# A graph layer on one core: two of three node pairs turned by VectorE, their blocks fetched in eight transfers, the straight pairs normalised by VectorE

## The reference

```python
msg = x[src]
agg = segment_sum(msg, dst, n)
deg = segment_sum(1, dst, n)
mean = agg / max(deg, 1)[:, None]
h = mean @ W_l + b + x @ W_r
u = x + h * sigmoid(h)
out = (u - mean(u)) / sqrt(var(u) + 1e-5)      # over a row's 512 features
```

## Time and profile before

| | |
|---|---|
| median of 3 runs (lowest to highest) | 1550.5 us (1549.07 to 1550.78) |
| the profiled execution: its own time, its span | 1550.07 us, 1548.2 us |
| mean granted TensorE clock | 0.989 of 2.4 GHz |
| busy shares of the span: PE, DVE, ACT, POOL | 97%, 85%, 77%, 67% |
| moved by DMA, mean rate | 397.68 MB, 257 GB/s |

### The profile page before, as it was taken

One profiled execution on the slowest core, in us unless ns is written; L12 is line 12 of the kernel. 1 busy time (PEld: TensorE's weight loads), 2 busy tenths in 40 slices (PEclk: granted clock), 3 DMA queues, 4 the chain that ended last, 5 costly groups with the idle time before them and its releaser, 6 DMA issues.

```text
span 1548.2 us, 23957 instructions
## 1 busy us (share of the span) xinstructions
PE 1501.8 (97%) x7198; PEld 1244.3 (80%) x7198; DVE 1319.6 (85%) x2088; ACT 1184.4 (77%) x1609; POOL 1030.7 (67%) x1097
## 2 busy tenths in 40 slices
PE   7799999999999899999999999999999999999996
PEld 6687778888887787888888888888888888888884
DVE  7699999999998777888888888888888888888886
ACT  4354433333334698999999999999999999999996
POOL 6466556656662766667767777677677776776673
PEclk9899999999999999999999999999999999999998
DMA  5656589989997689999999999999999999999995
GB/s 193 173 178 192 166 247 266 266 259 272 267 267 232 176 258 265 277 283 276 276 271 268 280 298 270 281 287 273 268 281 281 289 280 279 280 277 275 290 270 184
DMA packets 298965, 397.68 MB, mean 257 GB/s; under 512 B 42652, under 2 KB 144822, under 8 KB 298837
## 3 DMA queue, kind: packets, MB, share of 16 engines
q1 hardware_dynamic: 250855, 321.43, 69.6%
q0 software_dynamic: 46944, 74.22, 18.0%
q10 hardware_dynamic: 1038, 0.50, 0.1%
HBM read 335.97 MB, written 139.67 MB: 307 GB/s over the span
## 4 chain that ended last, share of the span: by engine, by line
PE 80%; ACT 5%; DMA 5%; issue 4%; DVE 4%; POOL 1%; SPq 1%; POOLq 0%; ACTq 0%; DVEq 0%
PE pH L529 72%; PE pT L633 4%; PE pT L602 3%; DMA cor<-correction_rows,node_idx 2%; ACT O L804 2%; ACT cor L750 1%; PE pT L540 1%; ACT pH L816 1%; DMA X<-in_x 1%; POOL cor L441 1%; DMA light_x<-in_x 1%; DVE Z L904 1%; ACT Z L828 0%; DMA xs<-in_x 0%; DMA wr_raw<-in_L_gnn_W_r 0%
## 5 line engine op out<-in xcount | busy, mean ns | idle before, releaser
L441 POOL DMA_INDIRECT cor<-correction_rows,node_idx x347 | 395.7, 1140 | 224.8 <-ACT cor L750 150.1
L529 PE MATMUL pH<-ws_hi,x_hi 128*128 128x512 f32 x876 | 348.3, 398 | 7.6 <-ACT pH L816 4.5
L529 PE MATMUL pH<-ws_hi,x_lo 128*128 128x512 f32 x876 | 343.9, 393 | 0.0
L529 PE MATMUL pH<-ws_lo,x_hi 128*128 128x512 f32 x876 | 343.4, 392 | 0.0
L529 PE MATMUL pH<-wb_hi,x_hi 128*128 128x512 f32 x688 | 276.1, 401 | 0.0
L529 PE MATMUL pH<-wb_hi,x_lo 128*128 128x512 f32 x688 | 268.9, 391 | 0.0
L529 PE MATMUL pH<-wb_lo,x_hi 128*128 128x512 f32 x688 | 268.5, 390 | 0.0
L804 ACT ACTIVATE O<-Z,shift,rstd 128x512 f32<-128x512 f32 x347 | 261.9, 804 | 3.6 <-DVE shift L1127 3.6
L1117 DVE BATCH_NORM_STATS2 stats<-Z 128x6 f32<-128x512 f32 x347 | 219.3, 673 | 0.3 <-issue 0.3
L1109 DVE TENSOR_TENSOR Z<-Z,X 128x1024 f32<-128x1024 f32 x174 | 211.2, 1214 | 2.8 <-ACT Z L828 2.8
L725 ACT ACTIVATE s_hi<-sums 128x512 fp32r<-128x512 f32 x98 | 62.0, 633 | 192.3 <-DVE sums L1028 192.3
(11 more groups left out here) (148 smaller groups left out, 2765.1 us busy)
## 6 DMA issues: line engine op xcount, KB each, us to landing
X<-in_x SPq DMA_DIRECT2D x173, 512.0 KB, 4.6
out<-O SPq DMA_DIRECT2D x173, 512.0 KB, 5.3
xs<-in_x SPq DMA_DIRECT2D x344, 128.0 KB
correction_rows<-c_out SPq DMA_DIRECT2D x98, 256.0 KB, 4.2
light_x<-in_x SPq DMA_DIRECT2D x58, 256.0 KB, 2.8
light_h<-early_product SPq DMA_DIRECT2D x44, 256.0 KB
out<-light_o SPq DMA_DIRECT2D x44, 256.0 KB, 4.3
join_row<-joined SPq DMA_DIRECT2D x98, 64.0 KB, 4.1
```

The source lines that it names most:

```text
L441: g.indirect_dma_start(out=out_, out_offset=None, in_=table, in_offset=bass.IndirectOffsetOnAxis(ap=idx, axis=0), bounds_check=bound, oob_ ...
L529: last = mm(ps, a[:, k], w[:, k], start=(n == 0 and not onto), stop=(n == len(terms) - 1), skip_group_check=onto)
```

## The change

Block pairs become two of every three (`t % 3 != 0`, apart from the last pair): 115 of the 174 instead of 86, which leaves 59 straight ones instead of 88. There are two pairs of raw and turned buffers, the second one in the tile `xd`. A block pair's 512 KB come in eight transfers, each of 32 rows, instead of four. In each of the eight the source is walked as 4 groups of features by 32 rows by 128 features, and the destination is all 128 partitions by 128 features; in each of the four it was 32 rows by 8 groups by 128 features on both sides, over 32 partitions. The normalisation of a straight pair moves from ACT (two activations) to DVE (two `tensor_scalar`), and DVE's shift for these pairs goes; it stays on ACT for block pairs. The waits are adapted: `blocks_in` has a semaphore for each buffer, and the normalisations wait for the pair before, since two engines now make them.

```diff
-        x_raw, x_blocks = xs[:, 0:2], xs[:, 2:4]
-        xd = [sb(f"xd{b}", [P, D], f32) for b in range(4)]
+        xd = sb("xd", [P, 4, D], f32)
+        x_raw, x_blocks = (xs[:, 0:2], xd[:, 0:2]), (xs[:, 2:4], xd[:, 2:4])
...
         def by_blocks(t):
-            return t % 2 == 1 and t < NP - 1
+            return t % 3 != 0 and t < NP - 1
...
             def load_blocks(t):
-                wait(sp, blocks_turned, (t + 1) // 2 - 1)
+                b, _ = block_ring(t)
+                wait(sp, blocks_turned, turned_by_dve(t) - 2)
                 first = BASE + 2 * t * P
-                for j in range(4):
-                    sp.dma_start(x_raw[32 * j:32 * j + 32].rearrange("r a (i c) -> r (a i) c", i=4),
-                                 x[first:first + 2 * P, j * P:(j + 1) * P].rearrange("(i r) c -> r i c", r=32)
-                                 ).then_inc(blocks_in, 16)
+                for i in range(8):
+                    sp.dma_start(x_raw[b][:, i // 4, i % 4 * P:(i % 4 + 1) * P],
+                                 x[first + 32 * i:first + 32 * i + 32].rearrange("r (j c) -> j r c", j=K)
+                                 ).then_inc(blocks_in[b], 16)
...
             def turn_blocks(t, q, u):
-                dve.wait_ge(blocks_in, 64 * ((t + 1) // 2))
-                if t > 1:
-                    dve.wait_ge(lo_made, t - 1)
-                v.transpose(x_blocks, x_raw).then_inc(blocks_turned, 1)
+                b, used = block_ring(t)
+                dve.wait_ge(blocks_in[b], 128 * (used + 1))
+                wait(dve, lo_made, t - 2)
+                v.transpose(x_blocks[b], x_raw[b]).then_inc(blocks_turned, 1)
...
+            def normalise(t, q, u):
+                if by_blocks(t):
+                    return
+                nt, rows = pair_shape(t)
+                b, used = ring(q, u, 2)
+                wait(dve, stored[b], 16 * used)
+                wait(dve, rstd_made, t + 1)
+                wait(dve, normed, t)
+                for a in range(nt):
+                    last = v.tensor_scalar(O[0:rows, b, a], Z[0:rows, u % 4, a], mv[0:rows, b, a, 0:1],
+                                           rstd[0:rows, b, a:a + 1], ALU.subtract, ALU.mult)
+                last.then_inc(normed, 1)
...
                 light(q, u)
+                shifted(t, q, u, -3, NP, normalise)
                 if by_blocks(t + 2):
                     single(t + 2, turn_blocks)
```

More of the change, by code:

```diff
@@ L175, in gnn_layer @@
         cor_in = [sem(f"cor_in{b}") for b in range(4)]
-        blocks_in, blocks_turned = sem("blocks_in"), sem("blocks_turned")
+        blocks_in, blocks_turned = [sem(f"blocks_in{b}") for b in range(2)], sem("blocks_turned")
         transposed, hi_made, lo_made, product, z_made, silu_made = (sem("transposed"), sem("hi_made"), sem("lo_made"),
@@ L205, in by_blocks, with turned_by_dve, block_ring @@
         def by_blocks(t):
-            return t % 2 == 1 and t < NP - 1
+            return t % 3 != 0 and t < NP - 1
         def turned_by_pe(t):
-            return t // 2 + 1 + t // (NP - 1)
+            return sum(not by_blocks(p) for p in range(t + 1))
+        def turned_by_dve(t):
+            return sum(by_blocks(p) for p in range(t + 1))
+        def block_ring(t):
+            n = turned_by_dve(t) - 1
+            return n % 2, n // 2
         def in_blocks(tile):
@@ L370, in edge_tile @@
                     load_blocks(1)
+                    load_blocks(2)
             peeled(0, ET, edge_tile)
@@ L447, in gather_xd @@
                 wait(pool, diff_made, t - 3)
-                gather(xd[u][:], x, dst_idx[:, t:t + 1], P, N - 1, xd_in[u])
+                gather(xd[:, u], x, dst_idx[:, t:t + 1], P, N - 1, xd_in[u])
             def gather_xs(t, q, u):
@@ L491, in make_rstd @@
                 wait(pool, mv_made, 2 * t + 2)
-                wait(pool, shift_made, t - 1)
                 wait(pool, normed, t - 1)
@@ L627, in transpose_x @@
                 pe.wait_ge(x_in[b], 16 * (used + 1))
-                if fixed(t) and t < 2:
-                    pe.wait_ge(sums_made, ET - 1 + t)
+                if fixed(t) and t < 4:
+                    pe.wait_ge(sums_made, min(ET - 1 + t, ET))
                 wait(pe, lo_made, t - 1)
@@ L788, in round_x @@
                 if by_blocks(t):
-                    act.wait_ge(blocks_turned, (t + 1) // 2)
-                    a_(in_blocks(x_hi[b]), x_blocks.rearrange("p a (i k r) -> p (a i) k r", k=K, r=32), ACT.Copy
+                    act.wait_ge(blocks_turned, turned_by_dve(t))
+                    a_(in_blocks(x_hi[b]), x_blocks[block_ring(t)[0]].rearrange("p a (i k r) -> p (a i) k r", k=K, r=32), ACT.Copy
                        ).then_inc(hi_made, 1)
@@ L798, in normalise @@
             def normalise(t, q, u):
+                if not by_blocks(t):
+                    return
                 nt, rows = pair_shape(t)
                 b, used = ring(q, u, 2)
-                wait(act, shift_made, t + 1)
+                wait(act, shift_made, turned_by_dve(t))
                 wait(act, stored[b], 16 * used)
+                wait(act, normed, t)
                 for a in range(nt):
@@ L1017, in subtract @@
                 wait(dve, turned, t - 1)
-                v.tensor_tensor(diff[b][:], xs[:, r], xd[r][:], ALU.subtract).then_inc(diff_made, 1)
+                v.tensor_tensor(diff[b][:], xs[:, r], xd[:, r], ALU.subtract).then_inc(diff_made, 1)
             def scan(t, q, u):
@@ L1079, in split_x @@
                 if by_blocks(t):
-                    v.tensor_tensor(in_blocks(x_lo[b]), x_blocks.rearrange("p a (i k r) -> p (a i) k r", k=K, r=32),
+                    v.tensor_tensor(in_blocks(x_lo[b]), x_blocks[block_ring(t)[0]].rearrange("p a (i k r) -> p (a i) k r", k=K, r=32),
                                     in_blocks(x_hi[b]).bitcast(f32), ALU.subtract).then_inc(lo_made, 1)
@@ L1114, in moments @@
                 wait(dve, u_made, t + 1)
-                wait(dve, rstd_made, t - 1)
+                if t > 1 and by_blocks(t - 2):
+                    dve.wait_ge(rstd_made, t - 1)
+                else:
+                    wait(dve, normed, t - 1)
                 for a in range(nt):
@@ L1178, in _ @@
             single(NP - 2, moments)
+            single(NP - 3, normalise)
             single(NP - 1, residual)
+            single(NP - 2, make_shift)
             single(NP - 1, moments)
-            single(NP - 2, make_shift)
             light_tail(light, NP, 4 * EARLY)
-            single(NP - 1, make_shift)
+            single(NP - 1, normalise)
             light_tail(light, 4 * EARLY, 4 * EARLY + 4)
```

## The result

| | before | after |
|---|---|---|
| median of 4 runs each, us (lowest to highest) | 1550.64 (1549.07 to 1551.23) | 1912.05 (1910.01 to 1912.73) |
| ratio, 95% interval | | 1.2329 (1.2311 to 1.2347) |
| profiled execution: own time, span | 1550.07, 1548.2 | 1910.01, 1908.2 |
| mean granted TensorE clock, of 2.4 GHz | 0.989 | 0.908 |

The change costs 362 us.

The account below looks back on a forecast made before the run. PE was taken as the bound, with ACT, DVE and DMA close below. Four engines' 883 us of blocks plus 708 us of the rest, 1591 against 1025, added 566 us to 1550.1: 2120 us, range 1930 to 2400.

Parts of the forecast that it names:

- four fixed engines: Block transfers, outermost count 4: the same four DMA engines carry all blocks; 1930 to 2400 us with a clock mostly holding, chance 0.80.
- rival of sixteen engines in effect: Block transfers spread over all 16 engines, PE stays the bound and 25.2 us come off: 1525 us, chance 0.08.
- both terms of the sum: Node stage, each of the four engines: 883 us of block packets at 30 ns plus 708 us of other transfers.
- The 24 ns by bytes: Lower price of a 512 B block packet, from 46.1 us for a MB in the edge stage; gives 1930 us.
- DVE's and ACT's shares: Node stage: DVE's added turning and normalising, 16.3 to 16.8 of 17.22 us in three pairs, and ACT's work, hidden under transfers.
- by itself this part costs nothing: DVE's added work in three pairs hides behind PE's matmuls if DVE waits for less than 0.9 us.
- PE's gain: Node stage: 29 pairs no longer turned by PE, 0.87 us each, 25.2 us off the bound if the rest keeps up.
- DMA's total: Rival with sixteen engines: 29 x 1024 more packets take 52 to 93 us, 1571 to 1612 us; chance 0.04 together with DVE.
- rival by DVE's waits: With sixteen engines DVE becomes the bound if its 15.5% of waits stays: +82 us, 1632; chance 0.04 together with DMA.
- the four are kept full: Blocks and loads of three pairs under way, about 27 us for one engine; SP's issues, 7.9 us at 0.49 each, hide.
- rival at 2530 us: PE's clock sits at 1.2 GHz while PE waits, at worst 11.5 us a pair; chance 0.07 together with crowding beyond 2400.
- The forecast signs: Node stage profile if right: PE at some 63%, DMA share from 0.97 to about 0.58, rate to about 190 GB/s.

Follow-up runs that it names:

- two-engine run: Changed kernel with each of its eight block transfers cut into two over 64 partitions, sixteen transfers of outermost count 2: 2646.64 us, one run.
- wide transfers: Changed kernel with each block pair fetched again in four transfers of outermost count 32 on both sides, into two buffers: 1603.21 us, ratio 1.0336.

## Why the prediction was right or wrong

**Right: four fixed engines.** "So a transfer runs on as many engines as divide its outermost count" holds in each run that bears on it: four closing packets for a transfer of the changed kernel, a share of 4 in 16 while blocks alone are under way, 309 us less with outermost 32, and twice the engine time with 2. That "the same four" carry them follows from the two-engine run. The rival of sixteen engines in effect is out. The Trainium skill (DMA: Bandwidth & Descriptors, Why a DMA increments its semaphore by 16 and not by 1) has this as its rule, and the counts of 2, 4 and 32 agree; which engines in the row they are, no run here shows.

**Wrong: both terms of the sum, too large.** "Each of the four engines has 115 x 256 x 30 ns = 883 us of blocks and 174 x 4.07 = 708 us of the rest." A packet takes 25 ns, by the slices and by the two-engine run: 736 us, 147 less. The stage measured 1025 + 362 = 1387 us (144 loads of `X` in 1150 us, 7.99 us a pair, agree with it), which leaves 651 for the rest, 3.74 us a pair, 57 less. Together 204, the whole of 2116 - 1912. The step that failed is the same in both: the shares of DMA time in the profile were taken for the time that an engine needs. They are times for which packets are held, and these overlap; for the rest this follows from the slices below alone. The 30 ns were right as held time, 29.6 in the changed kernel; an engine takes a packet every 25. The 24 ns by bytes were held time as well, of packets of 1165 B in the mean, so that end came near by luck.

**Wrong: the range.** It missed because the rest had an upper bound, 4.78, and no lower one. That 46.1 us for a MB are held time, and more than an engine needs, could be seen in the kernel before: its window of 580 to 590 us has a DMA share over one.

```profile
580.00:590.00 10.00, 10.00 (x49) 8.34 (x48) 8.38 (x16) 9.95 (x13) 7.79 (x10) 1.00 1.09 300
```

The slices of 393 GB/s in the changed kernel give 16 / 0.393 = 40.7 us for a MB, so (169.3 x 40.7 + 1037) / 16 / 135.8 = 3.65 us a pair. The trace of before has slices as fast, 385 to 427 GB/s in this window; they would have put the lower end at 115 x 256 x 24 ns + 174 x 3.65 = 1342 us, 1867.

**Right, and hidden as told: DVE's and ACT's shares.** "DVE's and ACT's shares are hidden under the transfers": ACT's normalisation in the changed kernel changes nothing. But "by itself this part costs nothing" holds only with the turn early and the blocks in time (1528 us); as written, with the turn at the end of its step, it is 1590 us even without traffic. The condition was DVE waiting "for less than 0.9 us in three pairs"; with wide transfers it waited 103 of 850 us, 2.25 in a triple of 18.6. One `tensor_scalar` took 0.58 us, above my 0.47 and below the 0.68 taken as the end:

```profile
L1155 DVE TENSOR_SCALAR O<-Z,mv,rstd 128x512 f32<-128x512 f32 x92 | 49.5, 579 | 0.0
```

**Right: PE's gain and DMA's total.** 25.2 us was forecast for PE, 1525; the two kernels without the block traffic end at 1522 and 1528. No kernel that fetches its blocks showed the gain. The rival by DMA's total said 1571 to 1612 for wide transfers, and these measured 1578 with ACT's normalisation and 1603 with DVE's. The rival by DVE's waits, 1632, came in no run; where DVE held the kernel, at 1590 us without the traffic, it was the turn's place in its queue.

**Right: the four are kept full.** The trace's packet records show fewer than four packets in flight for under 0.1% of 700 to 1850 us. But SP doesn't wait at `residual` any more, and that its issues take 0.49 us and hide was wrong: the full engines hold it up, and `X`, the stores and the early tiles behind it. **Half right: the clock.** It fell to 0.88 in the stage, between its two levels in the mean, and PE isn't what the chain waits for, so the rival at 2530 us did not come. The forecast signs, 63% of PE, a share of 0.58 and 190 GB/s, were those of a longer stage. In 1387 us the same work makes 72% at the full clock, 0.67 and 218; measured were 81% at the lower clock, 0.68 and 216.

**Open.** How much of the 25 us between DVE's and ACT's normalisation under full traffic (1602 and 1578) is DVE's time and how much its place in the queue wasn't separated. Nor was what the fetch costs by the total of the transfers from what it costs by their time to landing.

## What to carry to other kernels

Look at the outermost count of both sides of a transfer before its size or number: 4 there put a quarter of the engines to work and cost 309 us, while twice as many transfers cost nothing. Before work is moved to a second fetch, ask whether the DMA engines have room; at a share of 0.97 they did not, and PE's gain could not be had at either of the two larger shares of block pairs tried. Price a DMA engine's work by what it moves in a stretch in which it is at its limit, not by the time for which its packets are held. Give each term a bound on both sides, and when one removed cause changes little, remove two together.

## What the hardware showed that I had not expected

SP's queue is held up by few full engines: an issue of 64 KB to four engines took 761 to 855 ns in the median where one to sixteen took 434 to 438, and its floor is higher as well, 522 ns against 311. While four engines drained the blocks, everything behind them in the queue waited, though the share of 0.2 to 0.3 leaves twelve engines idle. And the share of DMA time in the profile can exceed one, 1.09 over 10 us and 1.02 over 800 us here, since an engine holds more than one packet at a time; a value near one isn't by itself a full set of engines.
